# A new order of work on all engines, a one-lag shorter pipeline and a transferred copy in a windowed transformer block

## The reference

```
xl = layernorm(tokens of x, 192 channels) * w1 + b1
xl = roll(xl, -3, -3); windows of 7 x 7 = 49 tokens, 64 windows an image
q, k, v = qkv projection (192 -> 576), 6 heads of 32 channels
out = softmax(q k' / sqrt(32)) v;  out = proj(out)        # per window
xl = windows back, roll(3, 3); layernorm * w2 + b2
h = fc2(gelu_exact(fc1(xl)))                              # 192 -> 768 -> 192
return h, as channels, + x
```

## Time and profile before

| | |
|---|---|
| runs | 2938.61, 2939.3, 2942.02 us; median 2939.3 |
| profiled execution | 2939.99 us, span 2938.2 us from first to last instruction |
| mean granted TensorE clock | 0.999 |
| TensorE busy | 2888.9 us, 98% of the span |
| VectorE, ScalarE, GpSimd busy | 92%, 92%, 46% |
| transfers | 213.11 MB, 606164 packets, 73 GB/s |

### The profile page before, as it was taken

How to read it: one execution, slowest core, us unless ns; L and a number is a source line. 1 busy time by engine, 2 the same in 40 slices (tenths; PEclk the granted TensorE clock), 3 DMA queues, 4 the chain that set the end, 5 groups by cost and what they waited for, 6 DMA issues and landing times.

```text
span 2938.2 us, 75046 instructions
## 1 busy us (share of the span) xinstructions
PE 2888.9 (98%) x26284; PEld 2820.7 (96%) x26284; DVE 2692.8 (92%) x7211; ACT 2689.2 (92%) x5500; POOL 1365.5 (46%) x1549
## 2 busy tenths in 40 slices
PE   4999999999999999999999999999999999999998
PEld 4999999999999999999999999999999999999998
DVE  7899999999999999999999999999999999999985
ACT  3899999999999999999999999999999999999996
POOL 3444444444444444444544444444445444444442
PEclk9999999999999999999999999999999999999999
DMA  5233333333333332333233233333333333333321
GB/s 111 61 76 75 70 75 75 74 68 78 77 70 71 74 78 68 75 78 70 71 74 78 69 73 79 70 69 77 78 70 71 76 76 69 75 75 73 69 60 26
DMA packets 606164, 213.11 MB, mean 73 GB/s; under 512 B 461411, under 2 KB 589156, under 8 KB 605796
## 3 DMA queue, kind: packets, MB, share of 16 engines
q1 hardware_dynamic: 601860, 206.64, 30.9%
q10 hardware_dynamic: 3936, 1.68, 0.3%
HBM read 130.69 MB, written 38.94 MB: 58 GB/s over the span
## 4 chain that ended last, share of the span: by engine, by line
PE 97%; DVE 1%; ACT 1%; SPq 0%; DMA 0%; issue 0%; POOL 0%; POOLq 0%; ACTq 0%
PE psum L318 8%; PE psum L319 7%; PE psum L320 7%; PE psum L322 7%; PE psum L321 7%; PE psum L600 7%; PE psum L574 6%; PE psum L554 5%; PE psum L565 5%; PE psum L555 5%; PE psum L566 5%; PE psum L556 5%; PE psum L580 4%; PE psum L328 4%; PE psum L330 3%; PE psum L329 3%
## 5 line engine op out<-in xcount | busy, mean ns | idle before, releaser
L1215 POOL TENSOR_TENSOR pr<-pr,rc 98x294 f32<-98x294 f32 x512 | 385.9, 764 | 382.3 <-DVE rc L1059 382.3
L756 ACT ACTIVATE hh<-psum,b 128x392 fp32r<-128x392 f32 x768 | 451.7, 588 | 46.2 <-PE psum L566 37.5
L759 ACT ACTIVATE hf<-psum,b 128x392 f32<-128x392 f32 x768 | 451.7, 588 | 6.3
L1188 POOL TENSOR_TENSOR ve<-mv,eps 98x4 f32<-98x4 f32 x256 | 80.9, 316 | 768.1 <-DVE mv L981 768.1
L1209 POOL TENSOR_TENSOR hl<-hf,hh 128x392 fp32r<-128x392 f32 x128 | 226.0, 1766 | 374.3 <-ACT hf L759 374.3
L1046 DVE TENSOR_REDUCE mx<-psum 98x6 f32<-98x294 f32 x512 | 232.3, 454 | 133.0 <-PE psum L575 129.0
L1023 DVE TENSOR_TENSOR hl<-hf,hh 128x392 fp32r<-128x392 f32 x640 | 347.7, 559 | 3.8 <-ACT hf L759 3.7
L318 PE MATMUL psum<-x_h,w_mh 128*128 128x392 f32 x768 | 275.0, 358 | 0.7 <-DVE pr L1051 0.6
L554 PE MATMUL psum<-hh,w2h 128*128 128x392 f32 x768 | 272.8, 355 | 0.0
L713 ACT ACTIVATE pt<-psum 113x294 f32<-113x294 f32 x512 | 207.1, 405 | 70.4 <-PE psum L580 70.2
L574 PE MATMUL psum<-km,qm 128*98 128x98 f32 x2048 | 261.0, 249 | 7.4 <-ACT qm L716 4.0
(11 more groups left out here) (144 smaller groups left out, 10410.3 us busy)
## 6 DMA issues: line engine op xcount, KB each, us to landing
bc<-mean_rstd SPq DMA_DIRECT2D x128, 392.0 KB, 3.7
vbd<-vs SPq DMA_DIRECT2D x1024, 36.8 KB
xg<-in_x SPq DMA_DIRECT2D x368, 96.0 KB, 2.4
xt<-in_x SPq DMA_DIRECT2D x112, 194.5 KB, 2.7
out<-xt SPq DMA_DIRECT2D x112, 194.5 KB, 1.9
xt<-in_x SPq DMA_DIRECT2D x112, 97.2 KB, 2.4
out<-xt SPq DMA_DIRECT2D x112, 97.2 KB, 2.1
xg<-in_x SPq DMA_DIRECT2D x128, 3.8 KB, 2.0
```

The source lines that it names most:

```text
L756: nc.scalar.activation(hh[:, m % HB, :], bank("fc1", m)[:, 0:T], ACT.Gelu, bias=b1[:, m:m + 1]).then_inc(s_hh, 1)
L759: nc.scalar.activation(hf[:, m % HB, :], bank("fc1", m)[:, 0:T], ACT.Gelu, bias=b1[:, m:m + 1]).then_inc(s_gelu, 1)
```

## The change

It has four parts. **Order:** the lists of pieces on TensorE, ScalarE, VectorE and GpSimd are replaced by other ones, with a new table of banks; TensorE's step now begins in the middle of a unit's second MLP product, its scores come one step after `qkv`, and the number of lags goes from 7 to 6. **Copy of o:** ScalarE writes the high part of the last 64 channels of `o` once instead of twice; the copy in `o_b` comes by a transfer, `copy_o`, issued by SyncE, and `project` waits for it. **Token layout:** the transposition takes 32 consecutive tokens for a block instead of every fourth, so the statistics have 104 partitions instead of 98 (the last eight tokens lie in block 3's place), and go out in four transfers instead of one. **Start:** VectorE and GpSimd take unit 0 up to its normalised input, and VectorE unit 1 up to its statistics, ahead of their loops; `other_weights` follows these.

```diff
-LAGS = 7
+LAGS = 6
@@ stats_out
-                sp.dma_start(spread_out[u % 2].rearrange("(p b) q -> p b q", b=PAIRS), mv[0][:, :, :]).then_inc(s_mr_out, 16)
+                for r in range(3):
+                    sp.dma_start(spread_out[u % 2, 128 * r:128 * r + 128].rearrange("(b t) q -> t b q", b=PAIRS), mv[0][32 * r:32 * r + 32]).then_inc(s_mr_out, 16)
+                sp.dma_start(spread_out[u % 2, 384:T], mv[0][96:LP[0], 0, :]).then_inc(s_mr_out, 16)
@@ SyncE
+            def copy_o(u):
+                sp.wait_ge(s_hi["o"], nth(u, 3, 2))
+                if u > 0:
+                    sp.wait_ge(s_pe["ln2"], nth(u - 1, 2, 1))
+                sp.dma_start(o_b[0:CR, :].bitcast(F32), o[2][0:CR, :].bitcast(F32)).then_inc(s_ob, 16)
@@ SyncE, loop over t: new order
+                spread(t - 3, 0); stats_out(t - 1); spread(t - 3, 1); copy_o(t - 4); stats_in(t - 1); store(t - 7) ...
-                stats_in(t - 2); spread(t - 4, 1); spread(t - 3, 0); stats_out(t - 1); store(t - 7) ...
@@ project
-                    claim(u, [("ln2", j // 2)], (s_lo["o"], 3, 2))
+                    claim(u, [("ln2", j // 2)], (s_lo["o"], 3, 2), *([(s_ob, 16, 15)] if j == 0 else []))
@@ hi_part, o
-                        for t in (o_b, o[2]):
-                            biased(o_rest(t, 0, wi), o_rest_psum(wi), bq[CR * wi:CR * wi + CR, 1:2], s_hi["o"])
+                        biased(o_rest(o[2], 0, wi), o_rest_psum(wi), bq[CR * wi:CR * wi + CR, 1:2], s_hi["o"])
@@ token_blocks
-                                    xg[:, u % XG].rearrange("p c (t b) -> p c b t", b=PAIRS)).then_inc(s_tr, 1)
+                                    xg[:, u % XG].rearrange("p c (b t) -> p c b t", b=PAIRS)).then_inc(s_tr, 1)
@@ VectorE, ahead of its loop
+            token_blocks(0); stats(0, 0, 0..3); mean_var(0, 0, 0..3)
+            less_mean(0, 0); times_rstd(0); lo_part("x1", 0, 0); lo_part("x1", 0, 1)
+            token_blocks(1); stats(0, 1, 0..3); mean_var(0, 1, 0..3)
+            other_weights(4)
@@ GpSimd, ahead of its loop
+            rstd(0, 0); less_mean_rest(0, 0); times_rstd_rest(0)
```

More of the change, by code:

```diff
@@ L462, in _ @@
                         stats_out(t - 1)
+                if 0 <= t - 3 < UNITS:
+                    spread(t - 3, 1)
+                if 0 <= t - 4 < UNITS:
+                    copy_o(t - 4)
+                if 0 <= t - 1 < UNITS:
+                    if t - 1 > 0:
+                        stats_in(t - 1)
                 if 0 <= t - 7 < UNITS:
@@ L622, in step @@
                 u = units(t)
+                if u[4] is not None:
+                    fc2_hi(u[4], 0)
+                    fc2_lo(u[4], 0)
+                    fc2_hi(u[4], 1)
+                    fc1(u[4], 4)
+                    fc2_lo(u[4], 1)
+                    fc2_hi(u[4], 2)
+                    fc2_lo(u[4], 2)
+                    fc1(u[4], 5)
+                if u[2] is not None:
+                    probs_t(u[2], 0)
+                    probs_t(u[2], 1)
+                if u[1] is not None:
+                    scores(u[1], 0)
+                    scores(u[1], 1)
+                if u[2] is not None:
+                    probs_t(u[2], 2)
+                    probs_t(u[2], 3)
+                if u[1] is not None:
+                    scores(u[1], 2)
+                    scores(u[1], 3)
+                if u[2] is not None:
+                    weighted(u[2], 0)
+                    weighted(u[2], 1)
+                    weighted(u[2], 2)
+                    weighted(u[2], 3)
+                if u[4] is not None:
+                    fc2_hi(u[4], 3)
+                if u[0] is not None:
+                    qkv(u[0], 4)
+                if u[3] is not None:
+                    x2_channels(u[3], 0)
+                    x2_channels(u[3], 1)
                 if u[0] is not None:
@@ L626, in step @@
                     fc2_lo(u[4], 3)
+                    fc2_hi(u[4], 4)
                 if u[0] is not None:
-                    qkv(u[0], 4)
+                    values(u[0], 1)
                 if u[4] is not None:
+                    fc2_hi(u[4], 5)
                     fc2_lo(u[4], 4)
+                if u[0] is not None:
+                    qkv(u[0], 3)
+                if u[4] is not None:
                     fc2_lo(u[4], 5)
                 if u[0] is not None:
[L633 to L642, removed]
+                    qkv(u[0], 2)
                 if u[2] is not None:
@@ L647, in step @@
                 if u[3] is not None:
-                    fc1(u[3], 2)
+                    fc1(u[3], 0)
                 if u[2] is not None:
                     project(u[2], 3)
-                if u[1] is not None:
-                    probs_t(u[1], 0)
+                if u[3] is not None:
+                    fc1(u[3], 1)
                 if u[0] is not None:
-                    qkv(u[0], 2)
+                    values(u[0], 2)
+                    values(u[0], 3)
                 if u[3] is not None:
+                    fc1(u[3], 2)
                     fc1(u[3], 3)
[L657 to L690, removed]
             steps(step)
@@ L855, in step @@
                     k_out(u[1], 0)
+                if u[5] is not None:
+                    y_low(u[5])
                 if u[2] is not None:
-                    pt_copy(u[2], 0)
+                    exps(u[2], 3)
                 if u[1] is not None:
@@ L1151, in step @@
                     row_max(u[3], 0)
+                    row_max(u[3], 1)
+                    less_max(u[3], 0)
+                    row_max(u[3], 2)
+                if u[0] is not None:
+                    if u[0] > 1:
+                        stats(0, u[0], 0)
+                if u[2] is not None:
+                    if u[2] > 0:
+                        lo_part("x1", u[2], 1)
+                if u[3] is not None:
+                    less_max(u[3], 1)
+                    row_max(u[3], 3)
+                    less_max(u[3], 2)
@@ L1152, in step @@
+                if u[0] is not None:
+                    if u[0] > 1:
+                        stats(0, u[0], 1)
+                if u[3] is not None:
+                    less_max(u[3], 3)
                 if u[6] is not None:
-                    hidden_lo(u[6], 3)
+                    hidden_lo(u[6], 4)
                 if u[3] is not None:
-                    less_max(u[3], 0)
-                    row_max(u[3], 1)
+                    row_sum(u[3], 0)
+                if u[4] is not None:
+                    lo_part("o", u[4], 0)
+                    o_rest_lo(u[4])
@@ new lines, in step @@
+                if u[0] is not None:
+                    if u[0] > 1:
+                        mean_var(0, u[0], 3)
+                if u[4] is not None:
+                    stats(1, u[4], 3)
+                    mean_var(1, u[4], 0)
+            token_blocks(0)
+            for j in range(PAIRS):
+                stats(0, 0, j)
+            for j in range(PAIRS):
+                mean_var(0, 0, j)
+            less_mean(0, 0)
+            times_rstd(0)
+            lo_part("x1", 0, 0)
+            lo_part("x1", 0, 1)
@@ L1170, in _ @@
+            token_blocks(1)
+            for j in range(PAIRS):
+                stats(0, 1, j)
+            for j in range(PAIRS):
+                mean_var(0, 1, j)
+            other_weights(4)
             steps(step)
```

251 lines of the change are left out of this document (114 added, 137 removed), and 10 rows, old and new, of the table BANK_USES.

## The result

The changed kernel takes 3022.7 us (3021.2 to 3026.7, five runs) where the kernel before takes 2939.9 beside it: 1.0279 times as long, 95% interval 1.0269 to 1.029. The forecast was 2935 with a range up to 2953. The profiled execution has a span of 3019.3 us.

The account below looks back on a forecast made before the run. The prediction took TensorE's row of products, 22.42 us a step, as the bound. From the median of 2939.3 us it summed steps 0, drain +1.4 less 1 and fill -4.7 to -4.3, or 2935 us, range 2922 to 2953.

Parts of the forecast that it names:

- The base: Steady steps: TensorE's row of products sets the time, and changed neighbours leave a step at 22.42 us.
- So I cost the new places at nothing; the cover is 0.5 us on each: Steady step: the new order causes no TensorE stalls, with the tightest spare 0.6 us, at weighted.
- The layout: One step of the new order laid out on TensorE's timeline, with VectorE's and ScalarE's results checked against it.
- Rival A: Steady step: GpSimd and VectorE hold each other up where newly side by side; +19 us, 2954; chance 0.20.
- The sign named for A: TensorE's list of waits would show hundreds of short waits for less_max or x_r.
- the sign named for being wrong: Steps differing from 22.42 us by over 0.05 us would show the forecast wrong.
- The rule cited for A: A VectorE instruction with two SBUF inputs and a GpSimd instruction that reads SBUF exclude each other.
- The transfer and ScalarE: Full step: o's transfer lands 2 to 2.5 us after issue, costing nothing; ScalarE sheds some 0.8 us, buying nothing.
- The transposition: Token-order transposition: 1.1 us instead of 1578 ns, by the DMA port rule near 0.8 us; only adds slack in steady steps.
- The start: Fill: x1(0) at 25.0, x1(1) at 50, first full step at 91.5 (88 to 97); -4.7 us.
- rival C: Fill: the prologue brings nothing, as weights and SyncE's queue set it, 97 instead of 91.5; 2940; chance 0.13.
- The drain: Last steps: o's transfer late by 0.7 us twice, +1.4, less 1 for old waits that go.

Follow-up runs that it names:

- e1: Changed kernel with VectorE's hidden_lo(2) moved from behind normalise(1) to ahead of normalise(0); 2941.9 us, 1.0012 of the kernel before.
- f1: e1 with the start's issues reordered: unit 0's statistics earlier, biases and second MLP weight on ScalarE's queue, projection's weights split last; 2938.5 us.
- f2: f1 with SyncE's issues held back until bc(0) has landed, and the first MLP weight issued from ScalarE's queue; 2938.5 us.
- d3: Changed kernel with hidden_lo(2) straight behind hidden_lo(1), ahead of the first norm's mean subtraction; 3001.2 us.
- e2: Changed kernel, order untouched, with hidden_lo(0), hidden_lo(1) and the first norm's mean subtraction replaced by same-shape passes of one SBUF input; 2943.6 us.
- e4: Changed kernel with the second copy of o made by ScalarE again and no transfer; 3023.5 us.
- e6: Kernel before, old order, with the transferred copy of o alone, issued ahead of the statistics' way in and the values' spread; 2943.1 us, 1.0003.

## Why the prediction was wrong

- **The base was right.** TensorE's row sets the step, and the new neighbours cost nothing: 22.41 us in e1, f1 and f2 where 22.42 was forecast.
- **The step that failed: "So I cost the new places at nothing; the cover is 0.5 us on each".** The layout held VectorE's and ScalarE's ends against five of TensorE's needs and left out `fc2_lo(2)`, which needs `hidden_lo(2)`. It had no row for GpSimd at all, and took every duration from where the instruction stood before. The root was 1.2 us there and is 2.6 here.
- **Rival A had the right mechanism, with the wrong victim, the wrong place and too small a price.** The prediction asked how much VectorE is held by GpSimd. Here GpSimd is held by VectorE first, and VectorE then waits for it. It looked at `scaled_probs`, `residual` and the remainder's passes, all large, and not at a root over four columns. One of these it did have right: `residual` holds `hidden_lo(2)` by 0.44 us. It allowed 0.15 us a step; it is 0.64. The sign named for A, short waits for `less_max` or x_r, did not come in the changed kernel (it came in d3, for `less_max`); the sign named for being wrong, steps off by over 0.05, did.
- **The rule cited for A is borne out in part.** The Trainium skill ("SBUF — State Buffer", Who interferes with whom) says that a VectorE instruction with at most one SBUF input, outside the 2-port modes, does not contend with GpSimd, and that one with two contends with a GpSimd instruction that reads SBUF; e2 agrees (root 1.01 us against 2.58). The Trainium skill ("SBUF — State Buffer", SBUF: two separate sides) also says that whichever instruction starts first gets the shared ports for the whole instruction; here the root started 0.29 us ahead of the passes by the profile and was the one held, while they kept their 0.52 to 0.56 us each. The measurement decides.
- **The transfer and ScalarE: right.** It lands 2.2 us after issue (2 to 2.5, from the earlier trace rows) and costs nothing in a full step (e4, e6). SyncE, which waited for `residual` before, now waits 612 us for `o` and 20 for `residual`; behind it nothing was late. ScalarE's relief buys nothing. The relief is 0.60 us a step, not 0.8.
- **The transposition: 0.97 us,** forecast 1.1 with 0.8 named beside it, and of no account in the steady part.
- **The start: mis-sized by 7.7 us,** 99.2 for 91.5 and outside its ends. `bc(0)` was issued 18.7 and landed 25.8, not 21: the four small statistics transfers had SyncE wait 3.9 us after the last issue where the single one before had it wait 1.7, and `bc(0)` then took 7.1 us to land beside loads and weights, where the median is 4.0. I had counted the issues and not the landings. This is 4.7 us for x1(0), but x1(1) is only 2.1 us late. Step 2 ends 4 us late, at 76.0 and not 72, since `project`, which waits for `copy_o(0)`, starts at 73.1 where I had it land at 69: SyncE's turns there, from one unit's `spread` to the next, took 16.3 and 14.5 us where I had 14. In step 3 TensorE's wait for `normalise` of unit 0, 5.2 us up to 81.2, makes `qkv` start at 87.4 and not 80. So without any stall the change would have come to 2942 (e1): the start's term is +3 and not -4.7, which is rival C and beyond its 97. The prediction's 2935 was too low even so.
- **The drain: right.** 61.9 us from the start of the first step without new input to the end of the span, forecast 62.9.

## What to carry to other kernels

When an order of work is laid out anew, lay out every engine, the half-idle one too, and go through all that the bound engine needs, with who produces it and what stands ahead of it in that queue. A duration read in one place is a duration beside its neighbours: of two engines that hold each other up, a 1 us instruction can take 2.6, and it is the wait for it that counts. Put work that is needed elsewhere into the time in which its engine waits anyway (e1: 81 us of 3023 by moving one line), but not where it has to wait itself (d3). Price a transfer by its landing from its turn in the queue.

## What the runs showed of the hardware

- GpSimd's reciprocal root over 98x4 numbers takes 1.01 us beside VectorE passes of one SBUF input, and 2.13 and 2.58 beside two and three VectorE passes of two SBUF inputs. Though it starts 0.29 us earlier, it yields to them and they don't get longer. It ends 0.87 us after the second or third pass; a fourth right behind (e1) made it no longer. A larger GpSimd pass does hold VectorE: in the changed kernel `hidden_lo(2)` took 1.00 us instead of 0.56 beside `residual`, which itself took 1.35 instead of 1.03.
- A 392 KB broadcast in the start took 8.3 us to land with the next loads and the projection's weights issued behind it and the first MLP weight ahead of it (f1), and 4.2 with that weight 1.7 us behind it and SyncE's issues held back until it had landed (f2). The DMA engines were over 0.9 busy in both.
- Four statistics transfers, three of 1 KB and one of 0.1 KB, kept SyncE waiting for 3.9 us after the last issue in the start, while others were under way; unit 1's four took 1.9.
